# A fourth output panel among layer 0's pairs, in a fused two-layer graph kernel

## The reference, cut to what matters

```python
# layer 0
A = 0.5 * adj with 0.5 added on the diagonal
h = relu((A / A.sum(axis=1)) @ x @ W.T + b)
x = layernorm(x + h)
# layer 1
xt = logmap0(x)                                      # a factor for each node
par = adj   * sigmoid(l_par[:, None] + r_par[None, :])   # l, r: xt @ halves of w_par
chi = adj.T * sigmoid(l_chi[:, None] + r_chi[None, :])
support = chi @ xt + par @ xt
x = layernorm(x + proj(expmap0(support)))
```

## Time and profile before

| | |
|---|---|
| median of 3 runs | 2200.4 us (2196.5 to 2200.65) |
| the profiled execution | 2200.13 us |
| its span, first to last instruction | 2198.3 us |
| busy TensorE / VectorE / ScalarE / GpSimd | 91% / 88% / 60% / 61% |
| transfers | 820.37 MB, mean 373 GB/s |

### The profile page before, as it was taken

The page is one execution under the profiler, slowest core; times in us unless marked ns, Lnnn a source line. Parts: engine busy times, 40 slices in busy tenths (PEclk is TensorE's granted clock), DMA queues, the critical chain, the costliest instruction groups (busy, mean ns, idle before and its releaser), DMA issues. The chain is left out here.

```text
span 2198.3 us, 18369 instructions
## 1 busy us (share of the span) xinstructions
PE 2006.2 (91%) x5072; PEld 898.4 (41%) x5072; DVE 1929.8 (88%) x1864; ACT 1318.0 (60%) x1508; POOL 1340.4 (61%) x639
## 2 busy tenths in 40 slices
PE   7999999999999998999999978898888888889886
PEld 3444444444444444444444433343333333334333
DVE  5757787988989989898999989999998998989896
ACT  0001324454464454454453588988989988989996
POOL 0000304534455554644544677999998998999996
PEclk9999999999999999999999988999999999999998
DMA  9978988989989989988989998999999999999993
GB/s 338 362 273 291 400 288 349 406 343 384 388 329 409 414 331 363 392 337 337 416 345 348 422 408 329 421 420 421 422 410 421 421 419 394 421 421 398 398 393 143
DMA packets 128453, 820.37 MB, mean 373 GB/s; under 512 B 14880, under 2 KB 27488, under 8 KB 31328
## 3 DMA queue, kind: packets, MB, share of 16 engines
q1 hardware_dynamic: 113392, 799.06, 90.7%
q10 hardware_dynamic: 14960, 20.13, 2.7%
HBM read 814.88 MB, written 4.26 MB: 373 GB/s over the span
## 5 line engine op out<-in xcount | busy, mean ns | idle before, releaser
L548 POOL TENSOR_TENSOR chi<-chi,ring 128x1024 f32<-128x1024 f32 x326 | 834.4, 2573 | 628.5 <-ACT chi L756 572.4
L1244 PE MATMUL ps<-keys,xtA 128*128 128x512 f32 x2048 | 981.3, 611 | 140.1 <-DVE keys L1045 110.5
L1171 PE MATMUL ps<-ring,xA 128*128 128x512 f32 x2048 | 918.4, 598 | 33.8 <-DMA xA<-in_x_g 15.2
L773 ACT ACTIVATE ps<-scores,prcr 128x1024 f32<-128x1024 f32 x492 | 544.2, 1106 | 394.2 <-DVE keys L1045 377.5
L1244 PEld LDWEIGHTS ps<-keys,xtA 128*128 128x128 f32 x2048 | 377.6, 193 | 683.8 <-issue 653.0
L935 DVE TENSOR_TENSOR dsum<-dsum,ring 128x2048 f32<-128x2048 f32 x240 | 594.1, 2475 | 30.4 <-DMA ring<-in_g_blk 24.4
L1171 PEld LDWEIGHTS ps<-ring,xA 128*128 128x128 f32 x2048 | 387.5, 192 | 519.1 <-issue 493.9
L1045 DVE TENSOR_TENSOR keys<-ps,chi 128x1024 f32<-128x1024 f32 x426 | 521.6, 1225 | 85.6 <-issue 31.3
L756 ACT ACTIVATE chi<-scores,prcr 128x1024 f32<-128x1024 f32 x426 | 483.8, 1136 | 16.3 <-DMA scores<-plcl_d 8.5
L1036 DVE TENSOR_TENSOR ps<-ps,ring 128x1024 f32<-128x1024 f32 x348 | 425.5, 1223 | 44.4 <-ACT ps L773 39.0
L548 POOL TENSOR_TENSOR chi<-chi,xA 128x1024 f32<-128x1024 f32 x79 | 185.7, 2366 | 18.4 <-ACT chi L756 18.4
(11 more groups left out here) (122 smaller groups left out, 820.9 us busy)
## 6 DMA issues: line engine op xcount, KB each, us to landing
ring<-in_g_blk SPq DMA_DIRECT2D x443, 1024.0 KB, 8.6
ring<-in_a_cols SPq DMA_DIRECT2D x190, 1024.0 KB, 10.0
xA<-in_a_cols SPq DMA_DIRECT2D x51, 1024.0 KB, 11.9
xA<-in_g_blk SPq DMA_DIRECT2D x44, 1024.0 KB, 10.0
scores<-in_a_cols SPq DMA_DIRECT2D x15, 1024.0 KB, 11.7
scores<-in_g_blk SPq DMA_DIRECT2D x15, 1024.0 KB, 10.7
scores<-plcl_d ACTq DMA_DIRECT2D x22, 512.0 KB, 10.4
xA<-in_x_g ACTq DMA_DIRECT2D x64, 64.0 KB, 11.8
```

The lines of the kernel that those rows point to most:

```text
L548: pool.tensor_tensor(out=chi(n), in0=chi(n), in1=half(t, n), op=ALU.mult).then_inc(m2_ready, 1)
L773: act.activation(dst, scores[:, row, 0, :], ACT.Sigmoid, bias=prcr[:, 2 * jt:2 * jt + 1]).then_inc(p_ready, 1)
L1171: ins = pe.matmul(Y[:, h * BANK:(h + 1) * BANK], xA[:, tile * D:(tile + 1) * D], t[:, tt * BP + h * BANK:tt * BP + (h + 1) * BANK], start= ...
L1244: ins = pe.matmul(outp[:, h * BANK:(h + 1) * BANK], xtA[:, jt * D:(jt + 1) * D], keys(n)[:, h * BANK:(h + 1) * BANK], start=begins, stop=i ...
```

## The change

`EARLY` becomes 4: panel 3 too has units among the pairs. `EARLY_ORDER` writes out the order of panels in rounds 4 and 6 so that panels 0 and 3 can share `scores[:, 0]`: their rows are fetched again when the buffer changes hands. What follows from the plan:

- Units 0 to 169 lie among the pairs, and every pair from 118 to 255 has one. There are 342 units behind the pairs.
- There are 30 groups instead of 26. Panel 3's first group has 32 units (96 to 127, at pairs 182 to 213). Copies out of `outp` fall in rounds 6 and 7 at pairs 216, 224, 232, 240 and 248; before they fell at 192, 200, 208, 224, 232 and 240. Behind the pairs they fall at units 171, 179, 187, 195, 203, 211, 219 and 227, and each is followed by an addition on GpSimd; before at 155, 163 and 171.
- Finals start at units 288, 316, 342, 368, 396, 422, 448 and 512; panels 0 to 3 are the ones not copied out of `outp` first.
- `taken` is no buffer of its own: sums go to the last panel's place in `xtA` until the last tangent is written, then to a place in `xA`; ScalarE's last tangent waits for the twelfth addition.
- `scores[:, 2]` is no longer a ring entry (10 in all). It holds a fifth `chi` buffer and a `par` buffer of own blocks. The fourth and fifth `chi` buffer come in at unit 207 (offset 37) instead of one more at unit 170 (offset 16). `APART` starts at offset 48 (unit 218) instead of 24 (unit 178).
- Rows of scores are fetched 14 times instead of 11.

```diff
-EARLY = 3
+EARLY = 4
+CB_MORE = 2
+EARLY_ORDER = {4: (3, 2, 1, 0), 6: (2, 3, 1, 0)}
+ENDS_BEHIND = {4: (0, 1), 5: (2, 3)}
 def early_groups():
...
-        for p in range(min(EARLY, a + 1)):
+        for p in EARLY_ORDER.get(a, range(min(EARLY, a + 1))):
...
-        if k - EARLY < EARLY:
-            order.append((k - EARLY, range((NPAN - 1) * TPP, UPP)))
+        for p in ENDS_BEHIND.get(k, ()):
+            order.append((p, range((NPAN - 1) * TPP, UPP)))
...
-            out.append((p - EARLY, base[p] + 34))
+        for i, q in enumerate(ENDS_BEHIND.get(p, ())):
+            out.append((q, base[p] + 28 + 26 * i))
...
-        if kind == "nat" and 2 * j == (ENDS[ROWS_GONE] + 16) // 2 * 2:
-            entries.insert(0, RING + EXTRA)
...
+TAKEN_LATE = [k for n, k in EVAC_AT_UNIT.items() if n >= LATE0 + 16]
+ADDED_BEFORE_TANGENT = ADDED[min(TAKEN_LATE)]
...
-MORE = LATE0 + 16
+MORE = ENDS[ROWS_GONE] + 8
-def buffer_of(n, few):
+def chi_buffer(n):
...
-    k = (n - MORE) % (few + 1)
+    k = (n - MORE) % (CB + CB_MORE)
...
-        taken = sb("taken", [P, BP])
...
-        own_par = [taken[:, :], xA[:, EXTRA * CH + BP:EXTRA * CH + 2 * BP]]
+        own_par = [scores[:, 2, 0, :], xA[:, EXTRA * CH + BP:EXTRA * CH + 2 * BP]]
+        def taken(k):
+            return own_par[1] if k in TAKEN_LATE else xtA[:, (NPAN - 1) * BP:N]
...
             def tangent(r):
                 act.wait_ge(fac_ready, r + 1)
+                if r == NPAN - 1:
+                    act.wait_ge(acc_added, ADDED_BEFORE_TANGENT)
...
-                    act.activation(taken[:, :], outp, ACT.Copy).then_inc(out_evac, 1)
+                    if k in TAKEN_LATE:
+                        act.wait_ge(l0_used, PAIRS)
+                        act.wait_ge(res_ready, NPAN)
+                    act.activation(taken(k), outp, ACT.Copy).then_inc(out_evac, 1)
```

More of the change, by code:

```diff
@@ L127, in finals @@
         out.append((p, base[p]))
-        if p - EARLY < EARLY:
-            out.append((p - EARLY, base[p] + 34))
+        for i, q in enumerate(ENDS_BEHIND.get(p, ())):
+            out.append((q, base[p] + 28 + 26 * i))
     return out
@@ L179 @@
 SLOT_OF_UNIT, SLOT_OF_NORMS, SLOT_OF_FINAL = slot_plan()
-ROWS_GONE = max(k for k, (p, _, a) in enumerate(GROUPS) if p == 2 and a < NPAN - 1)
 def load_plan():
@@ L219, in row_plan @@
 def row_plan():
-    out, use, end_of = {}, [0, 0, 0], [None, None, None]
-    buf = 0
+    out, use, holder, end_of = {}, [0, 0, 0], [None, None, None], [None, None, None]
+    late = 0
     for k, (p, tiles, a) in enumerate(GROUPS):
         if a < NPAN - 1:
-            b = p
-            if (p, "early") not in out:
-                use[b] += 1
-                out[(p, "early")] = (b, use[b], None)
-        else:
-            b = buf % 2
-            buf += 1
+            b = p % 3
+        else:
+            late += 1
+            b = late % 2
+        fetched = None
+        if holder[b] != p:
             use[b] += 1
-            out[k] = (b, use[b], end_of[b])
-        end_of[b] = ENDS[k]
+            fetched = end_of[b]
+        out[k] = (b, use[b], fetched)
+        holder[b], end_of[b] = p, ENDS[k]
     return out
@@ L240, in rows_of @@
 def rows_of(n):
-    k, p, _ = UNIT[n]
-    return ROWS_OF[(p, "early")] if GROUPS[k][2] < NPAN - 1 else ROWS_OF[k]
+    return ROWS_OF[UNIT[n][0]]
 def evac_plan():
@@ L265 @@
 ADDED_ALL = ADDED[-1]
+TAKEN_LATE = [k for n, k in EVAC_AT_UNIT.items() if n >= LATE0 + 16]
+ADDED_BEFORE_TANGENT = ADDED[min(TAKEN_LATE)]
 ROW_LOAD_AT = {}
 for _k, (_p, _t, _a) in enumerate(GROUPS):
-    if _a == NPAN - 1:
+    if ROWS_OF[_k][2] is not None:
         ROW_LOAD_AT.setdefault(ROWS_OF[_k][2] + 2, []).append(_k)
-MORE = LATE0 + 16
-def buffer_of(n, few):
+ROWS_GONE = max(k for k, (p, _, a) in enumerate(GROUPS) if p == 2 and a < NPAN - 1)
+MORE = ENDS[ROWS_GONE] + 8
+def chi_buffer(n):
     if n < MORE:
-        return n % few, n - few if n >= few else None
-    k = (n - MORE) % (few + 1)
-    return (few, n - few - 1 if n > MORE else None) if k == 0 else ((MORE + k - 1) % few, n - few - 1)
+        return n % CB, n - CB if n >= CB else None
+    k = (n - MORE) % (CB + CB_MORE)
+    before = n - CB - CB_MORE
+    return (CB + k, before if before >= MORE else None) if k < CB_MORE else ((MORE + k - CB_MORE) % CB, before)
 APART = {n for n in range(MORE + 8, UNITS) if n % 8 == 2 and n not in OWN_AT}
@@ L393, in adj_resnorm_kernel @@
         x_in = [sem(f"x_in{G}") for G in range(NG)]
-        r_in = [sem(f"r_in{e}") for e in range(RING + EXTRA + 1)]
+        r_in = [sem(f"r_in{e}") for e in range(RING + EXTRA)]
         l_in = [sem(f"l_in{k}") for k in range(3)]
@@ L478, in wait_free @@
                 if before is None:
-                    if e == RING + EXTRA:
-                        sp.wait_ge(c_ready, ENDS[ROWS_GONE] + 1)
-                        sp.wait_ge(p_ready, ENDS[ROWS_GONE] + 1)
-                    elif e >= RING:
+                    if e >= RING:
                         sp.wait_ge(l0_used, PAIRS)
@@ L556, in add_taken @@
                 pool.wait_ge(out_evac, k + 1)
-                pool.tensor_tensor(out=at, in0=taken[:, :], in1=at, op=ALU.add).then_inc(acc_added, 1)
+                pool.tensor_tensor(out=at, in0=taken(k), in1=at, op=ALU.add).then_inc(acc_added, 1)
             def norm_floor(k):
@@ L738, in passage @@
                     copy_rows(r)
-                if tick == T_LOADL and r < EARLY:
+                if tick == T_LOADL and r < 3:
                     load_rows(r, r)
@@ L747, in sigmoids @@
                 act.wait_ge(prcr_ready, jt // TPP + 1)
-                b, before = buffer_of(n, CB)
+                b, before = chi_buffer(n)
                 if before in APART:
@@ L752, in sigmoids @@
                     act.wait_ge(k_ready, SUMS[before])
+                elif b > CB:
+                    act.wait_ge(c_ready, ENDS[ROWS_GONE] + 1)
+                    act.wait_ge(p_ready, ENDS[ROWS_GONE] + 1)
                 elif b == CB:
@@ L762, in sigmoids @@
                     elif i == 1:
-                        act.wait_ge(l0_used, PAIRS)
-                        act.wait_ge(res_ready, NPAN)
-                    else:
-                        act.wait_ge(acc_added, ADDED_ALL)
+                        act.wait_ge(acc_added, ADDED_ALL)
+                    else:
+                        act.wait_ge(c_ready, ENDS[ROWS_GONE] + 1)
+                        act.wait_ge(p_ready, ENDS[ROWS_GONE] + 1)
                     dst = own_par[i % 2]
```

8 lines of the change are left out of this document (4 added, 4 removed).

## The result

The changed kernel took 2217.5 us (2215.34 to 2220.21, 4 runs) against 2199.06 us for the kernel before (4 runs). The ratio is 1.0086 with a 95% interval of 1.0068 to 1.0103: slower by 0.9%, clear of noise. The direction was forecast. The size was not: 2208 was predicted, with a range up to 2219, and +7.7 us expected where +18.4 was measured; 2217.5 lies in the part (2213 to 2222) that had a chance of 0.18. It was one of the faster ones of the changed kernel (2215.82 us where the median is 2217.5), which is most of what 15.7 lacks to 18.4.

What follows compares the result with a forecast made beforehand. TensorE was taken to set the pace among the pairs and GpSimd behind them; 39.4 - 37.1 + 9.3 + 3.3 - 8.7 + 1.5 = +7.7 us on 2200.1 gave 2208 us, range 2197 to 2219.

Steps and rivals of the forecast that it cites:

- term 6: Transfers behind the pairs: loads slower than GpSimd use up the ring's lead before unit 280, +1.5 us, bounds 0 and 5.7.
- term 1: Pairs: 16 more units in rounds 6 and 7, which then resemble rounds 4 and 5 with a copy stall, +39.4 us.
- term 5: Finals behind the pairs: fewer copied out first (-1.7 us) and a fifth `chi` buffer (-7), together -8.7 us.
- Term 4: Last passage: one more VectorE step waits for GpSimd (+2.1 us) and an `APART` unit's saving is lost (+1.2), +3.3 us.
- Terms 2 and 3: Behind the pairs: 16 units gone at 2.32 us each, -37.1 us; four added GpSimd additions that nothing hides, +9.3 us.
- Rival B: Stretch before unit 280: loads come late and later own blocks repeat it, +8 us, 2216; chance 0.18 with other added waits.
- Rival A: Finals: the fifth `chi` buffer makes them nearly gapless and the kernel faster, 2196 us; chance 0.13 together with D.
- Rivals C and D: C: pairs cost 32 us, time 2201, chance 0.19; D: both stages' freed time equal, 2196, 0.13 together with Rival A.

Runs made afterwards that it cites:

- section 2 and 3: Kernel before with a fifth `chi` buffer in place of the eleventh ring entry: span 2195.4 us; its control, only that entry taken away: 2198.3, against 2198.3.
- the merged version: Changed kernel with tiles 48 to 55 of panels 0 to 3 in the panels' last groups: span 2201.6 us, ratio 1.0015 to the kernel before.
- the merged version with more `APART`: The merged version with two units in eight in `APART` instead of one: ratio 1.0011 to the kernel before.

## Why the prediction was wrong, point by point

| term | predicted | measured |
|---|---|---|
| 1 pairs | +39.4 | +37.4 |
| 2 units gone | -37.1 | -37.1 |
| 3 additions | +9.3 | +9.3 |
| 4 last passage | +3.3 | -0.9 |
| 5 finals ahead of unit 448 | -8.7 | -1.9 |
| 6 offset 32 to the first final, rest | +1.5 | +6.2 |
| the final at 448 and the end | 0 | +2.5 |
| sum | +7.7 | +15.5 |

The measured column is made of the windows above and those of before (in term 6, 16.5 - 9.3 less the 1.0 that the same stretch had before; the rest to 15.7 is rounding). They are single executions: by the means given above, term 1 is +39.5. "Units gone" is arithmetic: 16 x 2.32, and 2.32 is still the pace where nothing waits.

**The failed step is term 5, and in it the sentence that GpSimd's 10.5 us behind `chi` in that buffer are there to be had, of which I took 7.** It added up waits and took them for a price. The fifth buffer did take the waits away, and the idle time was back a unit later in one piece. Four kernels show it from both sides: the fifth buffer is worth 2.1 us at the dense finals (53.3 and 51.2) and 2.0 at the wide ones (54.5 and 52.5), where I took 7. The other part of term 5, one final fewer of the kind that is copied out first, was set at -1.7. By kind a final left 10.0 and 7.8 us instead of 10.1 and 8.0, so the mix gave about what was forecast, and with the buffer's 2.1 the term would be -3.8. It came to -1.9, so some 2 us were lost again. One place is the eighth product of the finals that aren't copied out first (section 2 and 3). Another shows in the timelines. At the finals at 368 and 448, each 26 units behind another, GpSimd waited for 2.2 us ahead of the final's fourth product, and in the merged version, where 42 units lie ahead of the one at 448, for 0.36 us.

```profile
2033.34 2.35 POOL L556 TENSOR_TENSOR chi<-chi,ring 128x1024 f32<-128x1024 f32 x1 [0.22 <-ACT chi L769]
2037.91 2.37 POOL L556 TENSOR_TENSOR chi<-chi,ring 128x1024 f32<-128x1024 f32 x1 [2.21 <-ACT chi L769]
```

That is the changed kernel at the final at 448; merged, in its second execution:

```profile
2017.66 6.99 POOL L556 TENSOR_TENSOR chi<-chi,ring 128x1024 f32<-128x1024 f32 x3
2025.02 2.37 POOL L556 TENSOR_TENSOR xA<-xA,ring 128x1024 f32<-128x1024 f32 x1 [0.36 <-ACT xA L769]
```

I had named VectorE's shorter time to catch up and then priced it inside the six finals only. The seventh, at 448, lies 26 units behind its forerunner instead of 38 and was left out: the stretch behind unit 448 took 2.5 us longer, 2.2 of them in its first 26 units. That denser finals cause this is not shown. The same wait stands at the first final of the changed kernel (1.84 us), which has no final ahead of it, and in the merged version with more `APART` (2.21 us), where 42 units lie between. What sets it stays open.

**Term 6 was mis-sized**: +6.2 instead of +1.5. The mechanism was right for the larger part, and its upper bound of 5.7 was passed by a little. At units 282 and 283 GpSimd lost 4.4 us, and TensorE's turned block was waiting for its natural loads:

```profile
1582.96 0.50 PE L1276 MATMUL ps<-ident,ring 128*128 128x128 f32 x2 [0.81 <-DMA ring<-in_a_cols]
1585.45 0.70 PE L1276 MATMUL ps<-ident,ring 128*128 128x128 f32 x2 [1.99 <-DMA ring<-in_a_cols]
1587.92 0.70 PE L1276 MATMUL ps<-ident,ring 128*128 128x128 f32 x2 [1.77 <-DMA ring<-in_a_cols]
```

"The block turned on TensorE brings two loads less" was the wrong reason to go low: this block asks for four loads before its first unit. The rest of the 7.2 us that the stretch has beside the additions are small waits at units 202, 208 and 210, 2.5 us together, with two PSUM slots and no `APART` unit there; no run took them apart.

**Term 4 had the wrong sign:** -0.9 instead of +3.3, with all ten executions of the changed passage at 109.5 us or less. The log map's factor in the changed kernel, VectorE:

```profile
1365.72 2.09 DVE L1008 TENSOR_TENSOR small<-small 128x8 f32<-128x8 f32 x1
1367.85 0.17 DVE L1009 TENSOR_TENSOR small<-small 128x8 f32<-128x8 f32 x1
1368.05 0.17 DVE L1010 SCALAR_TENSOR_TENSOR small<-small 128x8 f32<-128x8 f32 x1
1368.25 0.20 DVE L1011 RECIPROCAL small<-small 128x8 f32<-128x8 f32 x1
1368.48 2.32 DVE L1012 TENSOR_TENSOR fs<-small 128x8 f32<-128x8 f32 x1
```

Two steps waited for GpSimd where three did before, and all nine steps together took 5.9 us instead of 8.0. The last step was one of the two that waited (2.32 us), as I had said of it. But the added copy on ScalarE (1.00 us) lay ahead of a `chi`, GpSimd paused for 0.64 us between two products, and three of VectorE's steps slipped through, two of them with two inputs. The rule about the shared port (the Trainium skill: SBUF — State Buffer, Who interferes with whom) agrees with each of these durations. It doesn't tell how many steps meet a GpSimd instruction. That depends on a pause of 0.64 us.

**Term 1 had the right number for a wrong reason.** I read two rounds that differ by 6.8 us and found a stall of 6.54 in the longer one. Taking two such stalls away gave back 0.5 us in three rounds together, and nothing at the first product behind them. Halving VectorE's degree sums took 25.8 us off the same three. So a full round is TensorE's 172 us, and VectorE, with 166 to 169 us of work, sets what comes on top. TensorE's stall was mostly where it waited for VectorE to catch up: it shrank from 6.6 to some 2 us when VectorE had less to do, and without it TensorE waited for loads. My sentence that TensorE sets the pace among the pairs holds for stretches without passage steps only. The comparison of rounds still carried, since it was made of whole rounds. What exactly rounds 5 and 7 have over 4 and 6 stays open. They have three and four of GpSimd's additions where the others have two and none, and GpSimd's instructions lengthen VectorE's, as the steps of term 4 show, but no run took those additions away.

**Terms 2 and 3** held. The first says why the change can't pay: a unit among the pairs cost 37.4 / 16 = 2.34 us in the profiled execution and 39.5 / 16 = 2.47 by the means, one behind them 2.32. The sixteen moved units are at best an even trade, and all that comes with them is loss. Rival B, late loads, was closest to what happened, and that its 2216 is so close is luck in part: of the 8 us by which the spans differ more than forecast, term 6 made 4.7, and the failed term 5 made 6.8. Rival A, with the sum hanging on the fifth buffer, was the trap I half stepped into; I also gave it a wrong time, since 20 us off my 2208 is 2188, and 2196 belongs to 12. Rivals C and D failed.

## What to carry to other kernels

A wait in a profile is a place, not a price: when three engines pass work around with few buffers between them, removing one wait moves the idle time one step on, and here it was less work on the chain's engines that shortened it ( 8.4 us for VectorE's relief, 2.1 for a buffer that removed 22 us of ScalarE's waits). Price a moved piece of work by whole stages that hold it and whole stages that don't, and test a stall's worth before naming it as the cause of their difference. When a schedule is made denser, follow it to the last place that it touches, and count the lead of loads as a stock that is used up: a block that asks for four loads at once is where it shows.

## What the runs showed of the hardware that wasn't expected

In the kernel with finals 26 and 54 units behind the first, units 202 to 209 took 3.1 us longer than with the same code in the changed kernel (23.8 and 20.6). In that stretch its granted TensorE clock was 0.76:

```profile
1392.00:1420.00 28.00, 22.70 (x51) 11.51 (x52) 21.40 (x21) 20.57 (x21) 22.95 (x10) 0.76 0.97 367
```

The changed kernel had 0.94 there:

```profile
1390.00:1418.00 28.00, 20.39 (x54) 9.11 (x55) 24.31 (x23) 23.57 (x24) 25.61 (x11) 0.94 0.99 371
```

Both are means of stretches at 1.2 and at 2.4 GHz. Just before, in the last passage, TensorE had been busy for only 75.8 of 109.2 us, and in the changed kernel for 76.5 of 109.4; the clock was 0.84 in both. The kernel with half of the degree sums and the copy first shows it again, with 22.6 us for units 202 to 209:

```profile
1358.50:1386.50 28.00, 22.54 (x53) 11.45 (x54) 22.56 (x22) 21.60 (x22) 23.71 (x11) 0.80 0.98 368
```

Six other executions with the same code in this stretch, the changed kernel among them, took 20.6 to 20.8 us. So when the clock comes back varies between executions of equal code, and here, with two PSUM slots and little slack, 2 to 3 us of it reached the time.

GpSimd's products started 2.46 us apart instead of 2.32 where they waited for loads at 421 GB/s, which is 1.05 million bytes in 2.49 us: transfers and GpSimd are so close behind the pairs that either can be the limit within the same 80 units.
